# The first attention's softmax, root and value steps, written another way

## What is computed

```
xn = layernorm(ctx);  ln = layernorm(layernorm(x))        # [64, 64, 128] each
q  = ln @ W_q;        k, v = split([xn ; ln] @ W_kv)      # 64 queries, 128 keys a batch
qn = rmsnorm(q, q_gamma) * 64**-0.5;  kn = rmsnorm(k, k_gamma)   # per head of 64
sim  = qn @ kn^T, masked keys set to -max                 # [64, 2 heads, 64, 128]
attn = softmax(sim);  out = (attn @ v) @ W_out + b_out
x = x + tanh(g_xattn[0]) * out
```

## Time and profile before

| | us |
|---|---|
| median of 3 runs | 1536.23 |
| lowest, highest | 1536.04, 1536.57 |
| profiled execution, span from the first to the last instruction | 1513.1 |
| busy in the span: PE / DVE / ACT / POOL | 1402.6 / 962.0 / 1013.7 / 520.6 |
| time of the profiled execution outside its span | not shown on its own |
| mean granted clock of PE | 0.981 |

### The profile page before, as it was taken

How to read it: one execution, slowest core, us unless ns; L and a number is a source line. 1 busy time by engine, 2 the same in 40 slices (tenths; PEclk the granted TensorE clock), 3 DMA queues, 4 the chain that set the end, 5 groups by cost and what they waited for, 6 DMA issues and landing times. The chain is left out here.

```text
span 1513.1 us, 33844 instructions
## 1 busy us (share of the span) xinstructions
PE 1402.6 (93%) x12061; PEld 1176.1 (78%) x12061; DVE 962.0 (64%) x2374; ACT 1013.7 (67%) x2018; POOL 520.6 (34%) x510
## 2 busy tenths in 40 slices
PE   5988799898999999999999999998899999979995
PEld 5887588777888888888888888887678888757874
DVE  6997767565666766766766666644345555556555
ACT  5887477566676676666666766663788887845552
POOL 3112245222222322322322321321233554555764
PEclk9999899999999999999999999998999999999998
DMA  8200100399990000000000000004000000013336
GB/s 222 84 1 1 57 2 1 66 160 123 20 113 2 1 2 2 2 2 2 2 2 2 2 2 2 2 1 128 1 21 13 15 16 17 18 36 84 93 96 187
DMA packets 124980, 60.46 MB, mean 40 GB/s; under 512 B 41945, under 2 KB 120241, under 8 KB 124690
## 3 DMA queue, kind: packets, MB, share of 16 engines
q1 hardware_dynamic: 120274, 48.92, 19.9%
q0 software_dynamic: 4544, 9.38, 1.9%
HBM read 28.84 MB, written 29.44 MB: 39 GB/s over the span
## 5 line engine op out<-in xcount | busy, mean ns | idle before, releaser
L1464 ACT ACTIVATE gelu<-psG,b_cols 128x512 f32<-128x512 f32 x256 | 176.3, 689 | 169.2 <-PE psG L142 157.9
L1570 PE MATMUL psDown<-w_down,hidden 128*64 128x128 f32 x4096 | 252.4, 276 | 0.8 <-DVE expert_out L1349 0.6
L1343 DVE SCALAR_TENSOR_TENSOR hidden<-psU,b_cols,gelu 128x512 f32<-128x512 f32 x256 | 189.6, 747 | 85.6 <-ACT gelu L1464 63.7
L1570 PEld LDWEIGHTS psDown<-w_down,hidden 128*64 128x64 f32 x4096 | 221.1, 137 | 18.9 <-DVE expert_out L1349 9.0
L1349 DVE TENSOR_TENSOR expert_out<-psDown,b_down 128x512 f32<-128x512 f32 x128 | 87.9, 686 | 148.8 <-PE psDown L1570 148.7
L1290 POOL TENSOR_TENSOR combine_sum<-combine_sum,combineT 128x512 f32<-128x512 f32 x48 | 61.3, 1278 | 332.1 <-ACT combineT L1478 332.1
L1319 POOL TENSOR_TENSOR dispatchT<-dispatchT,dispatch_inv 128x512 f32<-128x512 f32 x64 | 67.1, 1049 | 232.0 <-DVE dispatch_inv L1444 232.0
L1830 POOL TENSOR_TENSOR probs<-probs,row_sum 128x512 f32<-128x512 f32 x64 | 66.2, 1035 | 143.6 <-DVE row_sum L1943 143.4
L140 PE MATMUL psU<-slots_hi,w_up_hi 128*128 128x512 f32 x256 | 103.0, 402 | 5.7 <-DVE hidden L1343 5.6
L2007 ACT ACTIVATE probs<-psS,neg_max 128x128 f32<-128x128 f32 x256 | 91.2, 384 | 22.8 <-DVE neg_max L1940 22.4
L140 PE MATMUL psG<-slots_hi,w_gate_hi 128*128 128x512 f32 x256 | 104.1, 406 | 1.7 <-ACT max_c_row L1519 0.7
(11 more groups left out here) (402 smaller groups left out, 3448.9 us busy)
## 6 DMA issues: line engine op xcount, KB each, us to landing
sorted_x<-empty_rows SPq DMA_DIRECT2D x1, 12736.0 KB, 86.9
tile_rows<-sorted_x SPq DMA_DIRECT2D x78, 65.0 KB, 1.9
sorted_x<-empty_rows SPq DMA_DIRECT2D x1, 4544.0 KB, 33.5
expert_ys<-expert_y SPq DMA_DIRECT2D x16, 256.0 KB, 4.9
x<-in_x SPq DMA_DIRECT2D x8, 256.0 KB, 5.9
ctx<-in_ctx SPq DMA_DIRECT2D x8, 256.0 KB, 5.9
w_gate_raw<-in_L_ffn_Wg SPq DMA_DIRECT2D x1, 2048.0 KB, 10.6
w_up_raw<-in_L_ffn_Wu SPq DMA_DIRECT2D x1, 2048.0 KB, 15.8
```

Of the source, the lines that this page charges most:

```text
L1343: dve.scalar_tensor_tensor(hid[e][:, half, :], U[half][:], bcol[:, 1, 4 * ch + 2 * e + half:][:, 0:1], gel[half][:], ALU.add, ALU.mult).th ...
L1464: act.activation(gel[half][:], G[half][:], ACT.Gelu, bias=bcol[:, 0, 4 * ch + 2 * e + half:][:, 0:1]).then_inc(s["gelu"], 1)
L1570: last = pe.matmul(DN[e * SEQ:(e + 1) * SEQ, j, :], hid[e][:, half, b * SEQ:(b + 1) * SEQ], wd[:, 2 * ch + e, half, :], start=(half == 0 a ...
```

## The change

- Exponential: the shift on DVE goes. ACT takes the exponential straight from the score bank, one instruction per batch with the negated row maximum as bias and the row sum written along (`accum_out`). DVE keeps the maxima (both ahead) and the reciprocal of the row sums, which moves behind the first and the second sum of squares.
- Roots: square root and reciprocal become logarithm and exponential with scale -0.5, on ACT, for token scales, slot scales and root mean squares; the epsilon becomes a clamp of the sums (DVE). One table set that has both functions is loaded at the start; the one-element exponential goes. DVE still waits for the token scales at the same place (`token_scales`), though it works out none itself.
- Gates: their four loads are issued by ACT at the start, with the tanh behind them, ahead of the first scales.
- Inputs in quarters: kv_in of an odd batch has latents first and context second, so that the latents of two neighbouring batches are 128 columns in a row. The queries read them there and the third copy goes; the mask is written to the matching quarters.
- Order: on PE keys of both halves and queries come before the values; on ACT the squares come before the copy of the values, and the two root instructions before the copies of the transposed probabilities.
- Attended values: per batch and head one product of 64 value columns with 64 queries, into one bank; one copy to SBUF instead of two of half height.

```diff
@@ loads, SP @@
-            for g in range(4):
-                gate = ins["g_ffn" if g % 2 else "g_xattn"][g // 2:g // 2 + 1]
-                sp.dma_start(graw[:, g:g + 1], gate.partition_broadcast(P)).then_inc(s["gates_loaded"], 16)
@@ DVE @@
             def token_scales(h):
-                r = slice(h * OP, (h + 1) * OP)
-                for n, inv in enumerate((c.inv, cinv)):
-                    dve.wait_ge(s["inv_b"], 2 * h + n + 1)
-                    dve.reciprocal(inv[:, r], work[:, n, r]).then_inc(s["inv_done"], 1)
                 dve.wait_ge(s["inv_done"], 2 * h + 2)
...
+            def row_inverse(o, g):
+                r = half_of(g)
+                need(dve, s["exped"], OB * o + OB // 2 * (g + 1))
+                dve.reciprocal(rs[:, r], rs[:, r]).then_inc(s["row_inv"], 1)
...
                         need(dve, s["sim"], 2 * o + g + 1)
+                        need(dve, s["exped"], OB * (o - 1) + OB // 2 * (g + 1))
                         dve.tensor_reduce(nmax[:, r], S[:, r, :], AX.X, ALU.max, negate=True).then_inc(s["neg_max"], 1)
-                        need(dve, s["neg_max"], 2 * o + g + 1)
-                        dve.tensor_tensor(pr[:, r, :], S[:, r, :], over(nmax[:, r], P, 2), ALU.add
-                                          ).then_inc(s["shifted"], 1)
-                    for g in range(2):
-                        r = half_of(g)
-                        need(dve, s["exped"], 2 * o + g + 1)
-                        dve.tensor_reduce(rs[:, r], pr[:, r, :], AX.X, ALU.add).then_inc(s["row_sum"], 1)
-                        need(dve, s["row_sum"], 2 * o + g + 1)
-                        dve.reciprocal(rs[:, r], rs[:, r]).then_inc(s["row_inv"], 1)
                 if has_core(o) and h + 1 < OCTETS:
                     token_scales(h + 1)
...
                         dve.tensor_reduce(ss[:, r], square.rearrange("p b (h d) -> p b h d", h=HEADS), AX.X, ALU.add
                                           ).then_inc(s["sum_sq"], 1)
+                        if n < 2 and has_core(o):
+                            row_inverse(o, n)
                         if n == 0 and h + 1 < OCTETS:
                             ctx_hats(h + 1)
-                    need(dve, s["root"], h + 1)
-                    dve.tensor_scalar(root[:], root[:], RMS_EPS, None, ALU.max).then_inc(s["root_max"], 1)
-                    need(dve, s["root_max"], h + 1)
-                    dve.reciprocal(root[:], root[:]).then_inc(s["root_inv"], 1)
+                    need(dve, s["sum_sq"], 3 * h + 3)
+                    dve.tensor_scalar(ss[:], ss[:], DH * RMS_EPS * RMS_EPS, None, ALU.max).then_inc(s["clamped"], 1)
                     need(dve, s["root_inv"], h + 1)
@@ ACT @@
-            def roots(h):
+            def inverses(h):
                 r = slice(h * OP, (h + 1) * OP)
                 for n in range(2):
                     act.wait_ge(s["inv_a"], 2 * h + n + 1)
-                    act.activation(work[:, n, r], work[:, n, r], ACT.Sqrt).then_inc(s["inv_b"], 1)
+                    act.activation(work[:, n, r], work[:, n, r], ACT.Ln).then_inc(s["inv_log"], 1)
+                for n, inv in enumerate((c.inv, cinv)):
+                    act.wait_ge(s["inv_log"], 2 * h + n + 1)
+                    act.activation(inv[:, r], work[:, n, r], ACT.Exp, scale=-0.5).then_inc(s["inv_done"], 1)
+            for g in range(4):
+                gate = ins["g_ffn" if g % 2 else "g_xattn"][g // 2:g // 2 + 1]
+                act.dma_start(graw[:, g:g + 1], gate.partition_broadcast(P)).then_inc(s["gates_loaded"], 16)
+            act.wait_ge(s["gates_loaded"], 64)
+            act.activation(c.gates[:], graw[:], ACT.Tanh).then_inc(s["gates_ready"], 1)
+            act.preload_act_table_set(SET)
+            inverses(0)
...
             def probs_exp(o, g):
-                r = half_of(g)
-                need(act, s["shifted"], 2 * o + g + 1)
-                act.activation(pr[:, r, :], pr[:, r, :], ACT.Exp).then_inc(s["exped"], 1)
+                need(act, s["neg_max"], 2 * o + g + 1)
+                need(act, s["pt"], o)
+                need(act, s["probs_normed"], 2 * (o - 1) + g + 1)
+                for b in range(g * OB // 2, (g + 1) * OB // 2):
+                    act.activation(pr[:, b, :], S[:, b, :], ACT.Exp, bias=nmax[:, b:b + 1], accum_out=rs[:, b:b + 1]
+                                   ).then_inc(s["exped"], 1)
...
-                    act.activation(lat, X[:, OP:OB, :], ACT.Identity, bias=cols[:, 3:4], scale=cols[:, 2:3]
-                                   ).then_inc(s["kv_in"], 1)
...
                 if has_core(o) and h + 1 < OCTETS:
-                    roots(h + 1)
+                    inverses(h + 1)
...
                 if has_head(o):
-                    need(act, s["v_proj"], h + 1)
-                    need(act, s["av"], h - 1)
-                    act.copy(v[1 - par][:], T[:]).then_inc(s["v_copied"], 1)
                     square_keys(h, 1)
                     need(act, s["q_proj"], h + 1)
                     need(act, s["qt"], h)
                     act.activation(sq_q[:], X[:, OP:OB, :], ACT.Square).then_inc(s["squared"], 1)
+                    need(act, s["v_proj"], h + 1)
+                    need(act, s["av"], h - 1)
+                    act.copy(v[1 - par][:], T[:]).then_inc(s["v_copied"], 1)
+                    need(act, s["clamped"], h + 1)
+                    need(act, s["kn"], 2 * h)
+                    need(act, s["qn"], h)
+                    act.activation(root[:], ss[:], ACT.Ln, scale=1.0 / DH).then_inc(s["root_log"], 1)
+                    need(act, s["root_log"], h + 1)
+                    act.activation(root[:], root[:], ACT.Exp, scale=-0.5).then_inc(s["root_inv"], 1)
...
-                    act.copy(oT[0:DH, :, :], S[0:DH, :, 0:SEQ])
-                    act.copy(oT[DH:P, :, :], S[DH:P, :, SEQ:P]).then_inc(s["oT_ready"], 1)
+                    act.copy(oT[:], S[:, 0:OB // 2, :].rearrange("p b (t n) -> p (b t) n", n=SEQ)).then_inc(s["oT_ready"], 1)
@@ PE @@
                     keys(h, 0)
+                    keys(h, 1)
+                    for p in range(OP):
+                        last = pe.matmul(X[:, OP + p, :], kvin[:, 2 * p:2 * p + 2, :].rearrange("p b n -> p (b n)")[:, SEQ:SEQ + P], w_q[:], start=True, stop=True)
+                    last.then_inc(s["q_proj"], 1)
                     need(pe, s["x_new"], o)
                     for b in range(OB):
                         last = pe.matmul(T[:, b, :], kvin[:, b, :], w_kv[:, D:2 * D], start=True, stop=True)
                     last.then_inc(s["v_proj"], 1)
-                    keys(h, 1)
...
-                        last = pe.matmul(S[:, b, :], v[par][:, b, :], pT[:, b, :], start=True, stop=True)
+                        for hd in range(HEADS):
+                            r = slice(hd * DH, (hd + 1) * DH)
+                            last = pe.matmul(S[r, b // 2, b % 2 * SEQ:(b % 2 + 1) * SEQ], v[par][:, b, r],
+                                             pT[:, b, hd * SEQ:(hd + 1) * SEQ], start=True, stop=True)
```

More of the change, by code:

```diff
@@ L824, in body @@
                 if o == OCTETS - 1:
-                    dve.wait_ge(s["first_root"], 1)
-                    dve.reciprocal(c.inv[:, 0:OP], work[:, 0, 0:OP]).then_inc(s["first_aggr"], 1)
-                    dve.wait_ge(s["first_aggr"], OP + 2)
+                    dve.wait_ge(s["first_inv"], 1)
                     dve.wait_ge(s["tx"], OCTETS)
@@ L877, in body @@
                     for n, (src, square, r) in enumerate(parts):
-                        need(dve, s["root"], h)
+                        need(dve, s["root_log"], h)
                         need(dve, s["squared"], 3 * h + n + 1)
@@ L898, in body @@
                         x_hats(h + 1)
+                if o == OCTETS - 1:
+                    row_inverse(o, 0)
+                    row_inverse(o, 1)
                 if o == OCTETS - 2:
-                    dve.wait_ge(s["slot_root"], 1)
-                    dve.reciprocal(sinv[:], work[:, 2, 0:SLOT_TILES]).then_inc(s["slot_inv"], 1)
                     dve.wait_ge(s["slot_inv"], 1)
@@ L975, in body @@
                 if has_core(o) and h + 1 < OCTETS:
-                    roots(h + 1)
+                    inverses(h + 1)
                 elif o == OCTETS - 2:
                     act.wait_ge(s["slot_var"], 1)
-                    act.activation(work[:, 2, 0:SLOT_TILES], work[:, 2, 0:SLOT_TILES], ACT.Sqrt).then_inc(s["slot_root"], 1)
+                    act.activation(work[:, 2, 0:SLOT_TILES], work[:, 2, 0:SLOT_TILES], ACT.Ln).then_inc(s["slot_log"], 1)
+                    act.wait_ge(s["slot_log"], 1)
+                    act.activation(sinv[:], work[:, 2, 0:SLOT_TILES], ACT.Exp, scale=-0.5).then_inc(s["slot_inv"], 1)
                 if has_head(o):
-                    need(act, s["v_proj"], h + 1)
-                    need(act, s["av"], h - 1)
-                    act.copy(v[1 - par][:], T[:]).then_inc(s["v_copied"], 1)
                     square_keys(h, 1)
```

(32 more changed lines are left out.)

26 lines of the change are left out of this document (11 added, 15 removed).

## The result

| | before | after |
|---|---|---|
| median of four runs each, us | 1536.4 | 1564.39 |
| lowest, highest | 1536.04, 1537.03 | 1563.19, 1573.6 |
| profiled execution: own time, span | 1534.17, 1532.4 (second profile) | 1563.19, 1561.5 |
| first attention: last instruction ends at | 155.22 | 181.60 |
| first attention: first six octets, us each | 15.41, then 15.67 | 20.91, 20.10, 20.97, 20.10, 20.97, 20.09 |

The medians are 28.0 us apart; the ratio is 1.0186 (95% interval 1.0162 to 1.021), which is +28.6 us. The forecast was 1558 us with 1538 to 1565. The second profile of the kernel before was taken with the experiments (`before_again`), because the first one has 23 us between span and time and this one 1.8, near the 1.7 of the changed kernel.

What follows compares the result with a forecast made beforehand. The prediction took DVE (VectorE) to bound the first attention's octet, busy 14.48 of 15.66 us. It summed 1536.2 + 9.0 (longer chain) + 13.0 (lower TensorE clock) = 1558 us, chance 0.52, range 1538 to 1565.

Steps and rivals of the forecast that it cites:

- The chain: First attention: the dependency path through all four engines grows by 1.8 us an octet, +9.0 us over the stage.
- The octet of 17.45: Predicted first-attention period: attended values at 11.34 us after the mask matmul plus 6.11 onward, against 15.66 before.
- ctx_hat (1.02): Step on DVE between first row inverse and second sum of squares, taken as 1.02 us.
- I take 1.80: Attended values on PE: 32 passes with 64-column weights taken at 1.80 us, with 0.90 as lower bound, 2.02 before.
- shows no speed that needs the parallel running: Attended values: claim that the earlier tiled row, 32 passes at 0.056 us each, gave no sign of parallel running.
- The clock: PE's gap before the attended values, transposes alone for 4.7 us, lowers the granted clock: 2.6 us in five octets, +13.0.
- the values take 1.8 more, the bias rows 0.6, the probability transposes up to 0.9: Price of the lower PE clock in one octet: 2.4 to 3.3 us in sum, taken as 2.6.
- right moment: Reason for counting five octets with a lowered PE clock: the drop needs the right moment.
- Rival 1: TensorE's clock stays and only the chain grows: +9.0, 1545 us, or 1538 with values at 0.90; chance 0.29.
- Rival 2: Faster: engine sums decide, at DVE's wait for scales and second row inverse; octet 13.7, -14, 1522 us; chance 0.09.
- Rival 3: Table loads return between exponential and logarithm on ACT, two an octet at 1.30: octet 19.05, 1555 us; chance 0.05.
- The signs given: First attention: DVE idle before sum of squares, busy near 11.2 of over 17 us; transposes at 9.5; clock under 1.00.

Runs made afterwards that it cites:

- before_again: The kernel before, unchanged, run and profiled again with the experiments: 1534.17 us (one run).
- keep_clock: The changed kernel with ten filler identity products on PE between values and probability transposes and three ahead of the attended values: 1542.22 us, ratio 1.0029 to the kernel before.
- rinv_first: The changed kernel with both row inverses right behind the two maxima on VectorE, ahead of the wait for the scales: 1540.21 us, ratio 1.001 to the kernel before.
- best_fill: The changed kernel reordered (both exponentials ahead of the squares, row inverses right behind the maxima, among other moves), plus PE fillers: 1527.87 us, ratio 0.9922 to the kernel before.

## Why the prediction was right, and where its terms were off

**The chain, +9.0 forecast, 8.3 measured** (`keep_clock` against the second profile of the kernel before, stage end; 9.0 against the first profile, without the fall of the clock at 131 us). The octet of 17.45 came out at 17.47, but by luck: two errors nearly cancel, the transposes 0.79 later and the values 0.65 shorter, and the part behind the values was 0.1 shorter than worked out. Scales ready at 5.77 (measured 5.90), VectorE released at 5.80 (5.93), row inverse at 8.29 (9.10), transposes at 9.49 (10.28): the step that failed here is "ctx_hat (1.02)", since it took 1.74 beside POOL (96.70 to 98.44). From the transposes to the values it was 1.85 in both. Then the attended values, "I take 1.80", took 1.15. Both ends had been given, and the lower one, 0.90, was nearer. I had taken the 0.056 us of a pass in the earlier trace rows as the price with 64 moving columns too; but that row moves 128 columns for each pass, and with 64 it is 0.036, so the moving columns counted. And at the same 128 moving columns a full-width pass takes 0.126 (2.02 / 16), more than twice as long: that this row "shows no speed that needs the parallel running" was wrong, both its halves were at work already. The rule of the Trainium skill that I had put aside ("TensorEngine Tiling (Array Packing)", Key Properties: column tiles run in parallel) agrees with that. The 0.2 us that the prediction puts on a change of mode did not show: PE stands idle for 0.77 us ahead of the values before the change (100.14) and after it (161.46 above).

**The clock, +13.0 forecast, 18.1 measured.** The mechanism, its place and its cause were as said: the earlier trace rows showed a fall behind transposes alone, and the changed kernel has the same inside every octet. The size was off in both factors: six octets and not five, and 3.06 instead of 2.6 each. My list of what runs slower ("the values take 1.8 more, the bias rows 0.6, the probability transposes up to 0.9") was off inside too. Values and bias rows together lose 1.3 (3.05 us from the values to the key transposes, 1.74 in `keep_clock`), since the values lose 0.83 and not 1.8; the part behind them, which I had left out, loses another 1.3 (105.28 to 110.19 against 94.24 to 97.86): transposes of keys and queries at 1.11 and 1.06 instead of 0.66 and 0.60. That makes 2.6, the octets of 20.10; where the stretch began earlier the probability transposes lose 0.88 on top, the octets of 20.97. The gap ahead was 3.55 us where 2.9 had been worked out, with the hold-up; whether that made six falls of five is not shown, and no run shows the "right moment" for which I had taken five.

**The sum.** 9.0 + 13.0 = 22 forecast; 8.3 + 18.1 = 26.4 measured in the stage. The remaining 2.6 us of the profiled pair are in stages that the change does not touch; the first expert stage alone took 866.9 to 876.9 us over the twelve profiles of these kernels, so that is not resolved. `keep_clock` is only 4.5 us (1.8 to 6.9) over the kernel before in the timed runs, and 8.3 in the stage. The two profiled executions are 8.2 apart (1542.34, 1534.17), but 1534.17 is less than any of the 15 executions timed beside it (1536.15 to 1543.68); where those were longer is not shown.

**The rivals.** Rival 1 (the clock stays) describes `keep_clock`: the chain alone. Its 1545 is near 1542, yet it was not what the change did. Rival 2 named the right place for a gain, DVE's wait for the scales and the second row inverse; with that place mended (`rinv_first`) the octet was 15.53, because the copy of the values comes next, and it took four more moves to 14.83. Its 13.7 was not reached. Rival 3 did not happen: no table loads returned. Its sum was off as well: two loads of 1.30 on the chain of 17.45 are 20.05 and not 19.05. The signs given: DVE idle ahead of the sum of squares (2.94), transposes at 10.3 instead of 9.5, clock 0.79; DVE busy 12.5 us an octet in `keep_clock` and not 11.2, of which 1.1 is time in which it was held.

## What to carry to other kernels

When an edit takes work off the bounding engine, write out the one chain that crosses the engines before you believe the engine sums: here VectorE lost 3 us of work an octet (14.48 to 11.45 where nothing holds it) and the octet grew, because a wait that kept its place had a new step queued behind it. Look where PE will be alone with a few transposes; the price of the lower clock is paid by all that stands behind the gap, and was here 3.06 us an octet, against 1.80 for the delay. A part (the pairs) that is worth 0.87 in one loop may be worth nothing in its neighbour: ask who waits for it.

## What the runs showed that was not expected

**VectorE's tensor_scalar waited while GpSimd's tensor_tensor ran.** Four instructions of `ctx_hat` took 1.81 beside it and 1.11 without, the clamp 0.55 and 0.89 instead of 0.18 (`best_fill`, `rinv_first`); the whole wait is booked as busy time of VectorE. Reductions are not held: the sum of squares at 99.12 in the changed kernel took 0.65 with POOL's normalization starting at 99.27. The Trainium skill ("SBUF — State Buffer", Who interferes with whom) has this rule: such an instruction can take the port pair that the two engines share, one of them holds it for a whole instruction while the other is blocked, and a reduction on this chip never takes it. The runs agree. It had no place in the earlier trace rows, where `ctx_hat` starts when POOL is done.

**Column halves run beside each other.** 32 passes (16 products) of 64 weight columns and 64 moving columns take 1.15 us at full clock and 1.98 at half, against 2.02 at full clock for the 16 passes of 128 and 128 that they replace. Both move 2048 columns in all, so passes that ran one after the other at the pace of the full width would have needed 2.02.
